# A decoder kernel on one Trainium2 core: the softmax denominators of one cross-attention are inverted at 32 columns and spread afterwards

## The reference, cut to what matters

```python
qh = q.reshape(b * h, d // h, m)          # d = 64 rows, h = 8 heads: 8 rows a head, m = 256
kh = k.reshape(b * h, d // h, -1)
vh = v.reshape(b * h, c // h, -1)
qk = jnp.einsum('bdm,bdn->bmn', qh, kh) * scale
sm = jax.nn.softmax(qk, axis=-1)
ret = jnp.einsum('bmn,bcn->bcm', sm, vh)  # back to 64 rows x 256, added to x
```

## Time and profile before

| | |
|---|---|
| time, median of 3 runs | 929.91 us (927.98 to 932.51) |
| the profiled execution | 933.79 us, of which the span from first to last instruction is 931.8 us |
| PE busy | 764.7 us, 82% of the span |
| DVE busy | 551.0 us, 59% |
| ACT busy | 342.4 us, 37% |
| GpSimd busy | 259.0 us, 28% |

### The profile page before, as it was taken

The page is one execution under the profiler, slowest core; times in us unless marked ns, Lnnn a source line. Parts: engine busy times, 40 slices in busy tenths (PEclk is TensorE's granted clock), DMA queues, the critical chain, the costliest instruction groups (busy, mean ns, idle before and its releaser), DMA issues. The chain is left out here.

```text
span 931.8 us, 13411 instructions
## 1 busy us (share of the span) xinstructions
PE 764.7 (82%) x4289; PEld 478.0 (51%) x4291; DVE 551.0 (59%) x1334; ACT 342.4 (37%) x781; POOL 259.0 (28%) x334
## 2 busy tenths in 40 slices
PE   4888958999999999965558998899987259999980
PEld 1444536877566666642234555555554126655550
DVE  3789846533232222247589999999965525544544
ACT  1455434333232222214346656656554012222210
POOL 2343420510000000014633245544523202322232
PEclk8999967999999999986579999999897569999995
DMA  9355331380298988822100001010141059998926
GB/s 346 128 225 215 155 151 51 124 350 1 76 318 306 379 317 295 292 79 68 51 1 1 23 25 49 27 49 24 41 152 39 28 212 322 324 324 300 330 92 231
DMA packets 56148, 151.91 MB, mean 163 GB/s; under 512 B 7089, under 2 KB 36657, under 8 KB 50961
## 3 DMA queue, kind: packets, MB, share of 16 engines
q1 hardware_dynamic: 50752, 135.99, 41.3%
q0 software_dynamic: 5328, 15.08, 4.4%
HBM read 109.87 MB, written 41.17 MB: 162 GB/s over the span
## 5 line engine op out<-in xcount | busy, mean ns | idle before, releaser
L1232 PE MATMUL ps<-f_rg,f_xT 128*128 128x512 f32 (+1 forms) x276 | 111.6, 528 | 2.3 <-DMA f_rg<-w_routed 1.7
L1135 DVE TENSOR_TENSOR f_rh<-f_gate,ps 128x256 f32<-128x256 f32 (+1 forms) x69 | 26.0, 377 | 121.7 <-ACT f_gate L965 81.9
L2062 ACT ACTIVATE b_PX<-ps 128x512 f32<-128x512 f32 x128 | 72.7, 597 | 44.0 <-PE ps L2305 42.2
L1782 DVE TENSOR_REDUCE b_smax<-ps 128x4 f32<-128x1024 f32 x64 | 77.8, 1216 | 14.9 <-PE ps L2281 14.7
L2539 POOL DMA_INDIRECT y<-f_ys,f_to x47 | 45.1, 959 | 112.7 <-DVE f_ys L2588 111.0
L965 ACT ACTIVATE f_gate<-ps 128x256 f32<-128x256 f32 (+1 forms) x69 | 24.0, 348 | 122.8 <-PE ps L1232 122.3
L1232 PEld LDWEIGHTS ps<-f_rg,f_xT 128*128 128x128 f32 x276 | 52.6, 192 | 30.3 <-issue 23.7
L2305 PE MATMUL ps<-b_Q,b_Cx 100*128 100x256 f32 x256 | 56.0, 324 | 9.6 <-ACT b_PX L2062 6.4
L1530 POOL MEMSET b_half<- 128x1 f32 x1 | 0.1, 98 | 222.8 <-POOLq L66 222.8
L1255 PE MATMUL ps<-f_rd,f_rhT 128*128 128x256 f32 x230 | 60.9, 380 | 0.3 <-issue 0.3
L2281 PE MATMUL ps<-b_Cx,b_Q 96*128 96x512 f32 x128 | 48.4, 462 | 14.4 <-DVE b_smax L1782 7.7
(11 more groups left out here) (319 smaller groups left out, 1741.8 us busy)
## 6 DMA issues: line engine op xcount, KB each, us to landing
f_rg<-w_routed SPq DMA_DIRECT2D x23, 1280.0 KB, 6.9
rows<-a_blank SPq DMA_DIRECT2D x16, 1152.0 KB, 7.2
rw<-w_ffn SPq DMA_DIRECT2D x24, 704.0 KB
f_rw<-w_ffn SPq DMA_DIRECT2D x23, 704.0 KB
f_rd<-w_routed SPq DMA_DIRECT2D x23, 640.0 KB, 4.7
f_xs<-rows SPq DMA_DIRECT2D x47, 144.0 KB
f_yk<-y SPq DMA_DIRECT2D x8, 512.0 KB, 7.6
raw<-w_shared SPq DMA_DIRECT2D x10, 384.0 KB
```

Source lines behind the costliest of these rows:

```text
L1135: nc.vector.tensor_tensor(rh[u % 2][:, 0:n], gate[u % 2][:, 0:n], ps[:, u % 4, n:2 * n], ALU.mult).then_inc(r_h, 1)
L1232: mm = nc.tensor.matmul(ps[:, u % 4, 0:2 * n], xT[b % 2][:, c, :], rg[b % R_SLOTS][:, off:off + 2 * n], start=(c == 0), stop=(c == C - 1))
L1782: nc.vector.tensor_reduce(smax[t % 2][:, k // C, k % C, :], ps[:, FIRST:FIRST + 2, :].rearrange("p u (g n) -> p (u g) n", g=2), AX, ALU.ma ...
L2062: nc.scalar.activation(PX[g % RING][:].rearrange("p c m -> p (c m)"), ps[:, RETS + G_TURN[g] % 2, :], ACT.Exp, scale=XSC).then_inc(turn_re ...
```

## The change

The reciprocal is no longer taken of the denominators spread over 256 columns.

- `spread_ret` spreads the numerators alone (two products instead of four, one selector instead of two). Behind them four more products turn the denominators: `ret`, 128 x 128 of it at a time, is the stationary operand and 8 columns of the identity the moving one. The result has, for each column m on its partition, the 32 denominators (2 x 2 x 2 x 4), in 32 columns of bank `OUT` (`den_turned`).
- A new call `denominators(c_)` on DVE, placed before `take(e_)`, takes the reciprocal of these 128 x 32.
- A new call `keep_spread` on ACT, placed between `x_exp(a_,1)` and `keep_pT(e_,1)`, copies the numerators to SBUF (`spread`) and the reciprocals, each repeated 8 times, to `rwide` (128 x 256).
- A new call `spread_den(c_)` on PE, placed between `turn_max(b_,1)` and `weigh_values(a_)`, turns `rwide` back with two products against the identity into columns 256 to 511 of the bank (`den_spread`).
- `add_cross` waits for `den_spread` and multiplies `spread` with that bank; the rest of it is as before.

```diff
@@ -1398,8 +1398,10 @@
         VT = slots("VT", [P, C * SB, G4, VS])
         PX = [sb(f"PX{n}", [P, C, D]) for n in range(RING)]
         ret = sb("ret", [P, 2, D])
-        rden = sb("rden", [P, D])
-        selr = sb("selr", [P, 2, 64])
+        rden = sb("rden", [P, C, 2, 2, G4])
+        rwide = sb("rwide", [P, C, 16, 8])
+        spread = sb("spread", [P, D])
+        selr = sb("selr", [P, 64])
 
         loaded = sem("loaded")
         gathered = [sem(f"gathered{t}") for t in range(TILES)]
@@ -1456,7 +1458,10 @@
         turn_read = sem("turn_read")
         pvx_done = sem("pvx_done")
         ret_ready = sem("ret_ready")
-        ret_spread = sem("ret_spread")
+        den_turned = sem("den_turned")
+        rden_ready = sem("rden_ready")
+        den_spread = sem("den_spread")
+        ret_kept = sem("ret_kept")
         logits_ready = sem("logits_ready")
         logits_kept = sem("logits_kept")
         l_max = sem("l_max")
@@ -1659,10 +1664,8 @@
                 nc.vector.tensor_scalar(sel[:, :, 1, 0:2], bc(eye, 2, 2), 0.0, None, ALU.mult)
                 nc.vector.tensor_copy(sel[:, :, 1, 2], eye).then_inc(sel_set, 1)
                 nc.vector.tensor_copy(upper[:], KR[:, R_UP:R_UP + P])
-                for q in range(2):
-                    ins = nc.vector.tensor_copy(selr[:, q].rearrange("p (h j r) -> p h j r", h=2, j=G4),
-                                                ident.rearrange("p (j h q r) -> p q h j r", j=G4, h=2, q=2)[:, q])
-                ins.then_inc(selr_set, 1)
+                nc.vector.tensor_copy(selr[:].rearrange("p (h j r) -> p h j r", h=2, j=G4),
+                                      ident.rearrange("p (j h q r) -> p q h j r", j=G4, h=2, q=2)[:, 0]).then_inc(selr_set, 1)
 
             def clear_ctx(s):
                 nc.vector.memset(Cx[s][:].bitcast(F32), 0.0).then_inc(cx_cleared, 1)
@@ -1782,13 +1785,19 @@
                 nc.vector.tensor_reduce(smax[t % 2][:, k // C, k % C, :], ps[:, FIRST:FIRST + 2, :].rearrange("p u (g n) -> p (u g) n", g=2),
                                         AX, ALU.max, negate=True).then_inc(s_max, 1)
 
+            def denominators(t):
+
+                if t is None:
+                    return
+                dve.wait_ge(den_turned, t + 1)
+                nc.vector.reciprocal(rden[:].rearrange("p c k h j -> p (c k h j)"), ps[:, OUT, D:D + 32]).then_inc(rden_ready, 1)
+
             def add_cross(t):
                 if t is None:
                     return
-                dve.wait_ge(ret_spread, t + 1)
-                step.done(nc.vector.reciprocal(rden[:], ps[:, OUT, D:2 * D]))
-                step.wait()
-                nc.vector.tensor_tensor(crossed[:], ps[:, OUT, 0:D], rden[:], ALU.mult).then_inc(read_cross, 1)
+                dve.wait_ge(ret_kept, t + 1)
+                dve.wait_ge(den_spread, t + 1)
+                nc.vector.tensor_tensor(crossed[:], spread[:], ps[:, OUT, D:2 * D], ALU.mult).then_inc(read_cross, 1)
                 dve.wait_ge(read_cross, t + 1)
                 step.done(nc.vector.tensor_tensor(X[:, t, :], crossed[:], X[:, t, :], ALU.add))
                 step.wait()
@@ -1908,6 +1917,7 @@
                     set_masks()
                     clear_ctx(0)
                     add_rows(0)
+                denominators(c_)
                 take(front(e_))
                 if e_ == 0:
                     set_selectors()
@@ -2067,6 +2077,15 @@
                     return
                 act.wait_ge(pvx_done, (t + 1) * GROUPS)
                 nc.scalar.copy(ret[:], ps[:, OUT, :].rearrange("p (k m) -> p k m", k=2)).then_inc(ret_ready, 1)
+
+            def keep_spread(t):
+                if t is None:
+                    return
+                act.wait_ge(rden_ready, t + 1)
+                if t >= 1:
+                    act.wait_ge(read_cross, t)
+                nc.scalar.copy(spread[:], ps[:, OUT, 0:D])
+                nc.scalar.copy(rwide[:], bc(rden[:].rearrange("p c k h j -> p c (k h j)"), 3, 8)).then_inc(ret_kept, 1)
 
             def exp_logits(t):
                 if t is None:
@@ -2127,6 +2146,7 @@
                 keep_pT(e_, 0)
                 x_exp(a_, 0)
                 x_exp(a_, 1)
+                keep_spread(b_)
                 keep_pT(e_, 1)
                 x_exp(a_, 2)
 
@@ -2335,11 +2355,26 @@
                 if t == 0:
                     pe.wait_ge(selr_set, 1)
                 pe.wait_ge(ret_ready, t + 1)
-                for q in range(2):
+                for k in range(2):
+                    mm = nc.tensor.matmul(ps[64 * k:64 * k + 64, OUT, 0:D], selr[:], ret[:, k],
+                                          start=True, stop=True, tile_position=(0, 64 * k))
+                one = ident.rearrange("p (j h x) -> p h j x", j=G4, h=2)[:, :, :, 8]
+                for c in range(C):
                     for k in range(2):
-                        mm = nc.tensor.matmul(ps[64 * k:64 * k + 64, OUT, q * D:(q + 1) * D], selr[:, q], ret[:, k],
-                                              start=True, stop=True, tile_position=(0, 64 * k))
-                mm.then_inc(ret_spread, 1)
+                        at = D + c * 16 + k * 8
+                        mm = nc.tensor.matmul(ps[:, OUT, at:at + 8].rearrange("p (h j) -> p h j", h=2), ret[:, k, c * P:(c + 1) * P], one,
+                                              start=True, stop=True)
+                mm.then_inc(den_turned, 1)
+
+            def spread_den(t):
+
+                if t is None:
+                    return
+                pe.wait_ge(ret_kept, t + 1)
+                for c in range(C):
+                    mm = nc.tensor.matmul(ps[:, OUT, D + c * P:D + (c + 1) * P],
+                                          rwide[:, c].rearrange("p g r -> p (g r)"), ident, start=True, stop=True)
+                mm.then_inc(den_spread, 1)
 
             def count_in_front(t, at):
 
@@ -2406,6 +2441,7 @@
                 second_scores(b_, 2)
                 turn_probs(a_, 1)
                 turn_max(b_, 1)
+                spread_den(c_)
                 weigh_values(a_)
                 second_scores(b_, 3)
                 turn_xn(front(e_), 0)
```

## The result

The changed kernel takes 949.17 us (median of 4, 942.79 to 950.78) against 930.11 for the kernel before (927.98 to 932.51): a ratio of 1.0197, 95% interval 1.0160 to 1.0234. It is slower, as forecast, but by 19.1 us where 10.7 were summed up, and 1.2 us outside the range. The profiled execution took 950.78 us, of which the span is 948.8.

The account below looks back on a forecast made before the run. DVE was taken to bound the stage, busy 28.97 of 30 us, so its delays reach the kernel's end. Tile delays 2.2 + 1.2 + 3.6 + 1.8 + 1.2 + 0.7 = 10.7 us on 929.9 gave 940.6, range 932.5 to 948.

Parts of the forecast that it names:

- steps 1 to 5: Tile 3's chain: turned denominators, short reciprocal, late maxima, spreading back before the multiplication, `weigh_values` to `add_attention`; 1.20 us more.
- the dear end: Upper bound from `weigh_values` to `aT`: `weigh_values` keeps its 1.17 us and ACT its 0.39, 0.6 us more a tile.
- the sum: All eight tiles' delays added, 10.7 us more, giving 940.6 us, own range 936.5 to 944.4; chance 0.69.
- tile 7: nothing else runs, a bare chain: Last tile, from `spread_ret` to the multiplication: ends at 729.29 us against 728.63, 0.7 us more.
- rival C: Slower yet: the new waits could bring a clock dip in each of seven tiles, 6.4 us more, 947.0; chance 0.11.
- A: Faster: DVE's freed time counts, 1.4 us gained a tile on seven tiles, 920.8 us; chance 0.07.
- B: The same: PE hides the turned products and runs `weigh_values` beside `spread_den`, 3.6 us more, 933.5; chance 0.13.
- the deciding point: DVE's two new waits together under 1.4 us a tile would favour A; forecast were 0.65 + 1.27 and a third.

Follow-up runs that it names:

- x6: The kernel before with the four turning products added on PE ahead of `spread_ret`'s own, read by nobody: 923.90 us against 922.79, ratio 1.0017.
- x5: The kernel before with an unused DVE memory fill of 1.1 us ahead of `take`: 940.12 us against 927.95, ratio 1.0112.
- y2: The kernel before with idle products in PE's two waits for ACT, tiles 0 to 4 only: 924.02 us against 922.79, ratio 1.0011.
- x7: The changed kernel with idle products in three of PE's waits: 937.32 us against 927.95 for the kernel before, ratio 1.0080.
- c_slots: The changed kernel with the last tile's `denominators` call moved behind `take_slots(6)`: 935.84 us against 921.55 for the kernel before, ratio 1.0174.
- x1: The changed kernel with the last tile's `denominators` call moved behind `take_slots(6)`, in another set: 935.28 us against 919.96 for the kernel before, ratio 1.0172.
- x3: The kernel before with the reciprocal taken of 32 of the 256 columns and no new step or wait: 920.21 us against 919.96, ratio 1.0005.
- x4: The changed kernel with `denominators(c_)` directly ahead of `add_cross(c_)`: 929.21 us against 919.96 for the kernel before, ratio 1.0114.

## Why the prediction was right in sign and short in size

**Right: steps 1 to 5, at full clock.** By their own numbers, for tile 3: DVE's wait before the reciprocal 0.60 (forecast 0.65); the reciprocal 0.36 (0.35); the turned passes 1.06 (1.12), with 0.97 us of weight loads, 0.12 each; ACT's copies end at 619.09, before PE comes to `spread_den` at 620.35 (hidden, as said); the wait before the multiplication 1.40 (1.27); `weigh_values` starts behind `spread_den`, at 620.99; the wait before `add_attention` 0.38 (0.56); the tile 1.11 (1.20). Tile 0 waits 2.09 before the reciprocal (near 2 forecast); tile 5 waits 0.50 and not near 2, yet its price is as forecast, since `den_turned` sets it. The Trainium skill, "TensorE: Matmul & The Clock Gate", section "LDWEIGHTS (loading the stationary operand)", gives 107 ns for a load of 128 columns; the row has 121, between that and the 130 that was used. Right too is where the cost sits: x6 shows that PE's work is nearly free and x5 that DVE's delay is not. With tile 3's 1.1 put in for the three tiles that met a low clock, the waits sum to 2.1 + 4 x 1.1 + 1.7 + 1.2 + 1.2 = 10.6, against 10.7. Two slips of its arithmetic weigh nothing: tile 7's terms add up to 729.26 (0.6, not 0.7), and six times the 0.6 of the dear end is 3.6, not 3.4.

What reached the stage's end can be read from profiles at like clock (us; full clock in the first stretch but for one interval of y2 at 0.95, 0.94 and 0.86 for tiles 5 and 6):

| stretch | before (y2) | changed | more | predicted |
|---|---|---|---|---|
| `spread_ret` of tile 0 to that of tile 5 | 155.71 | 162.19 (x7) | 6.5 | 7.0 |
| on to that of tile 7 | 49.89 | 51.62 (c_slots) | 1.7 | 3.0 |
| on to the last `own` | 20.14 | 23.8 (changed) | 3.6 | 0.7 |

That is 11.8 against 10.7. It is near for a part by luck: tiles 5 and 6 pass on 1.3 less than was put down for them, and this hides nearly half of what the last turn costs more.

**Failed: the sum, by what it leaves out.** Two terms.

1. *The last turn*, in "tile 7: nothing else runs, a bare chain". What is queued behind the new wait was named as `take` and `maxima(b_,3)`, which holds in the turns of a full pipeline. In the last turn there is neither; there is `take_slots(6)`, and behind it GpSimd's scatters and tile 7's root. The last stretch took 3.6 us more where 0.7 was put down: 1.2 to the multiplication, and 2.4 behind it (2.4 to 2.9 by the tails with and without the move). Shown in the profiles; the timed runs don't resolve it.

2. *The clock, rival C.* It was held against the sum as another case, with a chance of 0.11, where it is a term that comes on top of it. The changed kernel ran at a lower mean clock than the kernel before in both repetitions, by 0.007 and 0.005 (each with an uncertainty as large as itself), and x1 and c_slots did so by 0.006 and 0.011. At 3.5 to 6.8 us for 0.01 that is 2 to 5 us. The size, one dip "in each of seven tiles", was too much: three tiles had one at the critical place. The mechanism is supported and not shown. For it: with PE's waits filled, 9.85 of 10 us busy, no interval between tiles 0 and 5 fell. Against it: a stretch of 10 us with PE busy 8.96 stayed at full clock, the kernel before has such dips too, and x3, without PE's new waits, ran 0.009 lower. The argument against C, "PE also gets more work per tile", didn't keep the clock up.

Together: 11.8 us by the profiles at like clock (10.4 to 10.9 by the line, 11.2 to 11.7 with the slope within the sets), and 2 to 3.5 more up to the 13.6 and 15.2 measured, which the lower clock can account for. Tile 1's rows show what it costs where it falls, 0.4 us on `turn_max` and on `weigh_values` each. That the mean clock is a cause of a whole execution's time and not only a companion is supported by the first set of fills; it is a rough measure.

That the time came out just beyond 948 hangs on the first measurement. With the repetitions' differences it would have been 943.5 and 945.1, inside the whole range and about at the upper end, 944.4, of that of the sum.

**Rivals A and B** are out. For A, the wait for PE was 0.60 + 1.40 against 1.4 freed, as the deciding point had it. x3 adds what the prediction could have read from the 0.24 us between `project_out` and DVE: even with no new wait, the freed time ends at the next input. B fell in both its parts: the turned passes took their own 1.06 us behind the spreading ones, and `weigh_values` began at 620.99, behind `spread_den` (from 620.35).

**Open:** the first measurement. Its four executions lie 14.4 us above the line, 3.5 more than the repetitions of the same kernel. The profiled execution of the kernel before, taken with it, lies 5.8 above too (933.79 against 928.0 at its clock of 0.904), so that chip may be slower at the same clock; no run tells. Nor is it settled how much of the fills' gain is real beyond the one set in which it was measured, or why x3's clock was low.

## What to carry to other kernels

A call in a hand-ordered queue holds up whatever stands behind its wait in *every* turn: go through the first and the last turn too, with the calls that only they have, not only through the full pipeline. Time freed on the busiest engine is worth no more than the slack of its next input, which is one row of the timeline (here 0.24 us of a reciprocal's 1.40). A wait that reaches PE may count twice, once as itself and once in the clock; a term for the clock belongs in the sum, with a range, and not only among the rivals. And the cost of a step in a pipeline is to be read in several tiles at the same clock: the one tile behind a slow interval made x4's order look free.

## What the runs showed of the hardware

- Products with 8 moving columns are no cheaper than their weights: eight passes took 1.06 us and their loads 0.97.
- Whole executions of one kernel differ in the mean granted clock: 0.895 to 0.923 in 64 of them, 915.5 to 935.8 us.
- The same code with the same busy time of PE, 8.96 of 10 us, ran at a granted clock of 0.71, 0.83 and 1.00 in three tiles of one execution.
- Idle products in PE's waits raised the mean clock by 0.022 in one set and 0.009 in the other, and the time gained was 5.8 and 1.2 us. They cost nothing in the intervals of tiles 1 to 4 (32.50 us) and came with 2 to 4 us more between tiles 5 and 7.
